# Graph network on one Trainium2 core: two edge stages regrouped into visits of 128-edge pairs, with unrolled gathers and an early fetch

## What is computed

```python
x = layernorm(x + L0(x))     # 4 rounds: segment_sum(x[src], dst), MLP with batch norms
x = layernorm(x + L1(x))     # edge MLP
x = layernorm(x + L2(x))     # 3 rounds of softmax aggregation (genconv)
x = layernorm(x + L3(x))     # continuous-filter interaction
# L1, per edge:  h = relu([x[src], x[dst], edge_attr_64] @ W1.T + b1)
#                agg = segment_sum(h @ W2.T + b2, dst);  then a two-layer node update
# L3, per edge:  Wij = (softplus(edge_attr_20 @ W_f.T + b_f) - log 2) * edge_weight
#                agg = segment_sum((x @ W_in.T + b_in)[dst] * Wij, src)
#                out = softplus(agg @ W_out.T + b_out) - log 2
```

## Time and profile before

| | |
|---|---|
| median of 3 runs | 3607.83 us (3603.68 to 3612.74) |
| profiled execution, its own time | 3592.89 us |
| its span, first to last instruction | 3591.2 us |
| prepare, adjacency and gin, up to the first layer norm | 0 to 741 us |
| edge_mlp: setup, loop, node update | 768 to 800, 800 to 1650, 1650 to 1702 us |
| genconv and its layer norm | 1725 to 2595 us |
| interaction: setup, loop | 2595 to 2661, 2661 to 3540 us |
| PE / DVE / ACT / POOL busy share of the span | 77% / 45% / 28% / 50% |

### The profile page before, as it was taken

The page is one execution under the profiler, slowest core; times in us unless marked ns, Lnnn a source line. Parts: engine busy times, 40 slices in busy tenths (PEclk is TensorE's granted clock), DMA queues, the critical chain, the costliest instruction groups (busy, mean ns, idle before and its releaser), DMA issues. The chain is left out here.

```text
span 3591.2 us, 51132 instructions
## 1 busy us (share of the span) xinstructions
PE 2767.2 (77%) x11270; PEld 1734.4 (48%) x11271; DVE 1627.7 (45%) x4686; ACT 999.8 (28%) x1815; POOL 1795.6 (50%) x1780
## 2 busy tenths in 40 slices
PE   3677788878999999998798899799636666666665
PEld 1233444457777777774444454354423333333333
DVE  7999222233333333332346436436524444444444
ACT  1333122221111111111110311211225454554543
POOL 2000000007777777772575475477037777777772
PEclk9999877765555555556899899899755555555556
DMA  0000000012222222221111011011021111111111
GB/s 7 3 0 0 20 0 0 0 49 55 53 53 54 55 53 53 54 54 38 31 17 12 11 17 13 10 17 17 28 87 35 35 35 35 35 35 35 35 35 32
DMA packets 181949, 108.52 MB, mean 30 GB/s; under 512 B 140291, under 2 KB 164066, under 8 KB 181148
## 3 DMA queue, kind: packets, MB, share of 16 engines
q0 software_dynamic: 88960, 66.98, 9.0%
q1 hardware_dynamic: 91662, 40.38, 4.4%
q10 hardware_dynamic: 1296, 0.79, 0.1%
HBM read 93.22 MB, written 13.33 MB: 30 GB/s over the span
## 5 line engine op out<-in xcount | busy, mean ns | idle before, releaser
L1720 POOL DMA_INDIRECT adj<-h_rows,adj x468 | 599.1, 1280 | 243.6 <-POOL adj L1716 124.9
L947 POOL DMA_INDIRECT work<-p_rows,work x468 | 569.4, 1217 | 242.8 <-POOL work L943 124.9
L1556 PE MATMUL ps<-adj,small 125*128 (+1 forms) x3150 | 631.5, 357 | 0.0
L1283 POOL DMA_INDIRECT edge_rows<-pay,small x425 | 513.6, 1208 | 129.2 <-issue 128.6
L1857 PE MATMUL ps<-adj 125*128 125x125 f32 x948 | 257.0, 442 | 313.1 <-DVE adj L1760 313.1
L1556 PEld LDWEIGHTS ps<-adj,small 125*128 125x128 bf16 x3150 | 311.5, 99 | 274.9 <-issue 12.6
L1857 PEld LDWEIGHTS ps<-adj 125*128 125x128 f32 x948 | 214.0, 326 | 399.2 <-DVE adj L1760 287.9
L1094 PE MATMUL ps<-small 64*125 64x128 f32 x936 | 337.2, 457 | 0.0
L928 POOL IOTA work<- 125x25 f32 x1 | 0.2, 154 | 656.7 <-POOLq L98 656.7
L986 DVE TENSOR_TENSOR work<-ps,work 125x384 f32<-125x384 f32 x156 | 87.1, 558 | 458.7 <-PE ps L1094 339.3
L1102 PE MATMUL ps<-work 125*128 125x125 f32 x936 | 249.3, 436 | 42.3 <-ACT work L1033 42.1
(11 more groups left out here) (318 smaller groups left out, 3727.4 us busy)
## 6 DMA issues: line engine op xcount, KB each, us to landing
small<-edge_attr SPq DMA_DIRECT2D x156, 93.8 KB
work<-p_rows,work POOLq DMA_INDIRECT x468
adj<-h_rows,adj POOLq DMA_INDIRECT x468, 3.4
edge_rows<-pay,small POOLq DMA_INDIRECT x425, 2.6
adj<-edge_rows SPq DMA_DIRECT2D x5, 996.1 KB
pay<-edge_pay SPq DMA_DIRECT2D x106, 46.9 KB
x_kept<-work SPq DMA_DIRECT2D x2, 1562.5 KB, 8.7
work<-x_kept SPq DMA_DIRECT2D x2, 1562.5 KB, 6.6
```

What stands on the lines that cost most here:

```text
L947: eng.indirect_dma_start(gathered[h][:, k * D:(k + 1) * D], None, p_rows[:, :], bass.IndirectOffsetOnAxis(ap=idx[h][:, k:k + 1], axis=0)). ...
L1283: eng.indirect_dma_start(edge_rows[:, :], bass.IndirectOffsetOnAxis(ap=place[:, k:k + 1], axis=0), pay[:, k * ROW:(k + 1) * ROW], None).th ...
L1556: ins = eng.matmul(ps[:, j, 0:cw], parts[k][:, i * D:(i + 1) * D], cols, start=first and i == 0, stop=last and i == 2, skip_group_check=True)
L1720: eng.indirect_dma_start(gathered[h][:, k * D:(k + 1) * D], None, h_rows[:, :], bass.IndirectOffsetOnAxis(ap=idx[h][:, k:k + 1], axis=0)). ...
```

## The change

- **Chunks, pairs, visits.** Edges are now in chunks of 128 (EW), two chunks make a pair (208 pairs, PAIRS). A *visit* is one pair with one node tile; a pair that touches two tiles is visited twice. Their number is fixed: 208 + 49 - 1 = 256 visits (VISITS) in edge_mlp with node tiles of 64 (MW, 49 of them), 208 + 25 - 1 = 232 (EDGE_VISITS) in interaction with tiles of 125. A word per visit (tile and pair) is computed at the start of each stage and read from SBUF by DVE, PE and SP with `value_load` at every visit. The tables of `prepare` (`ranges`) and its bin ends go.
- **One flat loop.** `quads_of` runs 4 visits (KB) per turn; the two-level loops `walk` and `units` go.
- **Gathers.** POOL's loop is written out, 208 pairs with 2 indirect DMAs each, the indices read straight from SBUF: no copy of indices, no wait for one. A ring of 4 pairs (edge_mlp) or 8 (interaction); POOL signals a pair's arrival two pairs later.
- **edge_mlp arithmetic.** The one-hot matrix by node and the edge features are stacked in one 128-row operand (`kmat`): SP fetches the targets of a pair broadcast over 64 partitions and the features under them, DVE turns the upper half into ones and zeros with one comparison, PE needs one matmul per chunk against the stacked weights (`qw`). The transposes, their copies, the bf16 splits and ACT's widening go. DVE adds each visit's sum into `R`.
- **interaction arithmetic.** Softplus as max(z, 0) + log(1 + exp(-|z|)), with exp and log from one ACT table; SP copies the edge rows of a visit; DVE adds each visit's sum into `S`.
- **Early fetch.** The layer norm ahead of interaction now fetches `edge_rows` (two transfers of 128 partitions, on SP and ACT) and the stage's weights. `h_rows` is written from two queues.

The core of the diff:

```diff
-            def body(w, c, q, opens):
-                for h in HALVES:
-                    if not first_of_all(q):
-                        eng.wait_ge(s_add[h], q)
-                        eng.nop(nofuse=True)
-                    eng.tensor_copy(idx[h], src_i[:, bass.ds(c + h * UH, UH)]).then_inc(s_idx[h], 1)
-                    eng.wait_ge(s_idx[h], q + 1)
-                    eng.nop(nofuse=True)
-                    for k in range(UH):
-                        eng.indirect_dma_start(gathered[h][:, k * D:(k + 1) * D], None, p_rows[:, :],
-                                               bass.IndirectOffsetOnAxis(ap=idx[h][:, k:k + 1], axis=0)
-                                               ).then_inc(s_g[h], 16)
+            for g in range(PAIRS + LAG):
+                if g < PAIRS:
+                    if g >= RING:
+                        n = eng.value_load(done[0:1, g - RING:g - RING + 1], min_val=1, max_val=VISITS)
+                        eng.wait_ge(s_add, nc.s_assert_within(n, 1, VISITS) + 2)
+                        eng.nop(nofuse=True)
+                    for k in range(PAIR):
+                        at = (g % RING * PAIR + k) * D
+                        c = g * PAIR + k
+                        eng.indirect_dma_start(gathered[:, at:at + D], None, p_rows[:, :],
+                                               bass.IndirectOffsetOnAxis(ap=src_i[:, c:c + 1], axis=0)
+                                               ).then_inc(s_g[g % RING], 16)
+                if g >= LAG:
+                    eng.wait_ge(s_g[(g - LAG) % RING], 16 * PAIR * ((g - LAG) // RING + 1))
+                    eng.nop(nofuse=True).then_inc(s_gd, 1)
...
+            def hots(v, b, word, i):
+                g, w = pair_of(word), tile_of(word)
+                eng.wait_ge(s_km[b], i)
+                eng.nop(nofuse=True)
+                eng.tensor_scalar(kmat[b][0:MW, :], kmat[b][0:MW, :].bitcast(I32), node_id[:, bass.ds(w, 1)], None,
+                                  ALU.is_equal).then_inc(s_ht, 1)
+                eng.wait_ge(s_tot, v + 1)
+                eng.nop(nofuse=True)
+                for k in range(PAIR):
+                    ins = eng.tensor_scalar(hot[b % 2][:, k * MW:(k + 1) * MW], iota, tile_lo[:, bass.ds(w, 1)],
+                                            dst_f[:, bass.ds(g * PAIR + k, 1)], ALU.add, ALU.is_equal)
+                ins.then_inc(s_hot, 1)
+            def add(v, b, word):
+                g = pair_of(word)
+                eng.wait_ge(s_gd, g + 1)
+                eng.wait_ge(s_prod, v + KB + 1)
+                eng.wait_ge(s_tot, v + 1)
+                eng.nop(nofuse=True)
+                eng.tensor_tensor(rows[b % 2], PROD[b % 2],
+                                  gathered[:, bass.ds((g & (RING - 1)) * (PAIR * D), PAIR * D)],
+                                  ALU.add).then_inc(s_add, 1)
+            def collect(v, b, word):
+                w = tile_of(word)
+                eng.wait_ge(s_tot, v + 3)
+                eng.wait_ge(s_r, v + 2)
+                eng.nop(nofuse=True)
+                r = R[:, bass.ds(w * MW, MW)]
+                eng.tensor_tensor(r, r, SUM[b % 2], ALU.add).then_inc(s_r, 1)
+            def body(v0, first, end):
+                words = {0: load_visit(eng, v0)}
+                if first:
+                    hots(0, 0, words[0], 32)
+                else:
+                    words[-1] = load_visit(eng, v0 - 1)
+                for b in range(KB):
+                    v = v0 + b
+                    if b < KB - 1 or not end:
+                        words[b + 1] = load_visit(eng, v + 1)
+                        n = (v0 // KB if isinstance(v0, int) else v0 >> 2) + (b + 1) // KB
+                        hots(v + 1, (b + 1) % KB, words[b + 1], n * 32 + 32)
+                    add(v, b, words[b])
+                    if b or not first:
+                        collect(v - 1, (b - 1) % KB, words[b - 1])
...
+            def hots(v, b, word):
+                g, w = pair_of(word), tile_of(word)
+                eng.wait_ge(s_tot, v + 1)
+                eng.nop(nofuse=True)
+                eng.tensor_scalar(rel[b], row3[:, bass.ds(g * PAIR, PAIR), SRC_C], tile_lo[:, bass.ds(w, 1)], None,
+                                  ALU.subtract).then_inc(s_rel, 1)
...
+            def message(v, b, word):
+                g = pair_of(word)
+                eng.wait_ge(s_ln, v + 1)
+                eng.nop(nofuse=True)
+                eng.scalar_tensor_tensor(soft[b], PROD[b], 0.0, soft[b], ALU.max, ALU.add).then_inc(s_sp, 1)
+                eng.wait_ge(s_sp, v + KB + 1)
+                eng.wait_ge(s_gd, g + 1)
+                eng.nop(nofuse=True)
+                eng.scalar_tensor_tensor(msg[b], soft[b], -LOG2,
+                                         gathered[:, bass.ds((g & (SLOTS - 1)) * (PAIR * D), PAIR * D)],
+                                         ALU.add, ALU.mult).then_inc(s_msg, 1)
...
+            if fetch:
+                fetch_rows(G, fetch, eng, 0, s_fetch)
+                eng.wait_ge(s_fetch, 16 * 8)
...
+            if fetch:
+                fetch_rows(G, fetch, eng, 1, s_fetch)
...
+            eng.wait_ge(s_spare, 2)
+            eng.dma_start(edge_rows.rearrange("(p c) f -> p c f", p=EW)[E % EW:EW, PAIR * PAIRS - 1, :],
+                          spare).then_inc(s_spared, 16)
+            eng.wait_ge(s_spared, 16)
```

More of the change, by code:

```diff
@@ L130, in build @@
         phase(genconv)
-        phase(layernorm)
-        phase(interaction)
+        rows = interaction_store(G)
+        phase(layernorm, fetch=rows)
+        phase(interaction, rows)
         phase(layernorm)
         phase(store)
-def load_range(nc, eng, ranges, row, w, steps, size):
-    word = eng.value_load(ranges[0:1, bass.ds(w + NT * row, 1)], min_val=0, max_val=(NC << 8) + steps)
-    return nc.s_assert_within(word >> 8, 0, NC), nc.s_assert_within(word & 255, 1, steps)
-class Passed:
-    def __init__(self, nc, eng, steps):
-        self.nc, self.eng, self.top = nc, eng, NT * steps
-        self.register = eng.alloc_register(f"steps_{nc.get_next_instruction_name()}")
-        eng.reg_mov(self.register, 0)
-    def now(self):
-        return self.nc.s_assert_within(self.eng.snap(self.register, min_val=1, max_val=self.top), 1, self.top)
-    def add(self, steps):
-        self.eng.reg_add(self.register, self.register, steps)
 def first_of_all(q):
@@ new lines, in total, with body @@
+            def total(v, b):
+                eng.wait_ge(s_hot, v + 1)
+                eng.wait_ge(s_relu, v + 1)
+                eng.wait_ge(s_r, v + 1)
+                eng.nop(nofuse=True)
+                for k in range(PAIR):
+                    ins = eng.matmul(SUM[b % 2], rows[b % 2][:, k * D:(k + 1) * D], hot[b % 2][:, k * MW:(k + 1) * MW],
+                                     start=k == 0, stop=k == PAIR - 1)
+                ins.then_inc(s_tot, 1)
+            def body(v0, first, end):
+                if first:
+                    products(0, 0)
+                for b in range(KB):
+                    if b < KB - 1 or not end:
+                        products(v0 + b + 1, (b + 1) % KB)
+                    total(v0 + b, b)
@@ L1591, in _, with interaction_store @@
                 eng.nop(nofuse=True).then_inc(s_fin, 1)
-def interaction(G):
-    nc, a, sem, work, small, ranges, ident, ps, T = (
-        G[k] for k in ("nc", "a", "sem", "work", "small", "ranges", "ident", "ps", "T"))
-    h_rows, edge_rows = G["h_rows"], G["edge_rows"]
+def interaction_store(G):
+    free = Words(G["adj_words"])
+    rows_t = free(EW, PAIR * PAIRS * ROW)
+    last, done = free(TP, 2, I32), free(1, PAIRS, I32)
+    w_in, b_in, w_out, b_out = free(D, D), free(EW, D), free(D, D), free(D, 1)
+    return dict(free=free, rows_t=rows_t, last=last, done=done, w_in=w_in, b_in=b_in, w_out=w_out, b_out=b_out)
@@ new lines, in collect, with body @@
+            def collect(v, b, word):
+                w = tile_of(word)
+                eng.wait_ge(s_tot, v + KB + 1)
+                eng.wait_ge(s_r, v + 2)
+                eng.nop(nofuse=True)
+                r = S[:, bass.ds(w * P, P)]
+                eng.tensor_tensor(r, r, SUM[b % 2], ALU.add).then_inc(s_r, 1)
+            def body(v0, first, end):
+                words = {}
+                if not first:
+                    words = {k: load_visit(eng, v0 + k) for k in (-2, -1)}
+                for b in range(KB):
+                    v = v0 + b
+                    words[b] = load_visit(eng, v)
+                    hots(v, b, words[b])
+                    message(v, b, words[b])
+                    if b >= 2 or not first:
+                        collect(v - 2, (b - 2) % KB, words[b - 2])
+                if end:
+                    for b in (2, 3):
+                        collect(v0 + b, b, words[b])
@@ L1817, in _, with body @@
+            def body(v0, first, end):
+                if first:
+                    attributes(0, 0)
+                    attributes(1, 1)
```

(9 more changed lines are left out.)

917 lines of the change are left out of this document (447 added, 470 removed).

## The result

The changed kernel takes 3739.1 us (median of 4 runs, 3737.17 to 3745.45) against 3607.8 before: ratio 1.0366, 95% interval 1.0348 to 1.0384. It is slower by 3.7%, and it lies above the range of the prediction. On a later occasion the ratio was 1.0381 (1.036 to 1.0402).

The account below looks back on a forecast made before the run. The prediction took POOL's stream to bound both loops before, PE also edge_mlp, and DVE's stream after. Its terms, +2 +15 -46 +3 +5 -6 = -27 us, gave 3580 us against 3607.8; range 3340 to 3700.

Parts of the forecast that it names:

- What bounds the kernel now: Before the change, POOL's instruction stream is full in both loops; in edge_mlp PE is full too, 805 of 850 us.
- POOL*'s term: Gather stream in both loops: 416 gathers in place of 468, 631 to 693 us, giving 219 and 222 us back.
- DVE becomes the long stream: edge_mlp's loop: DVE's reads and register work on every visit, 3.31 us x 256; 852 us against 850.
- Interaction: Interaction's loop: DVE's visit 3.45 us, 3.83 with the top of the turn, x 232; 894 us against 879.
- Setup of interaction and the layer norm: Ahead of interaction's loop: early fetch cuts the setup by 46 us; the layer norm that hides it grows by 3.
- Rest: Other stages: edge_mlp's setup +5 us for the table of visits, prepare -6 for about 30 small operations fewer.
- A: Both loops, slower: hand-overs cost more, 0.15 us per visit, 3653 us; up to 0.25, 3702; chance 0.30.
- B: Both loops, faster: DVE's register work runs beside the engine, 3130 us, or 3359 if only in edge_mlp; chance 0.15.
- C: Both loops: a contended load of a word takes 0.6 us, +0.45 per visit, 3800 us; chance 0.03.
- D: No difference: the early fetch only moves its cost into the third layer norm, 3596 to 3608 us; chance 0.05.

Follow-up runs that it names:

- before_128: Kernel before, its gathers fetching 128 rows in place of 125 (three unused rows) in edge_mlp and interaction: 3429.0 us, ratio 0.9525.
- fetch_alone: Changed kernel, with the early fetch moved into a stage of its own between the layer norm and interaction: 3720.0 us.
- half_gathers: Changed kernel without the second gather of each pair in edge_mlp, from the fifth pair on: the stretch with edge_mlp lasted 1025.4 us.
- lean: Changed kernel, DVE's words split once and kept, over the end of a turn too, without DVE's range checks on them: 3436.1 us, ratio 0.9572.
- more_reads: Changed kernel with one more, unused read of a word by DVE in every visit of both loops: 4039 us.
- carry: Changed kernel, DVE keeping the words of its last two visits in registers over the end of a turn, in both loops: 3641.8 us, ratio 1.0102.
- gather_sizes: Changed kernel, edge_mlp's gathers fetching eleven numbers of rows in turn, from 128 to 32: 3773 us.
- gather125: Changed kernel, edge_mlp's gathers fetching 125 rows in place of 128: 3814 us.

## Why the prediction was wrong

**What bounds the kernel now** was right, and before_128 shows it: cheaper gathers alone took 175 us off, interaction by 137, and edge_mlp came to rest on PE.

***POOL*'s term** was wrong in size, without effect on the time. I carried 1.217 and 1.280 us over to gathers of 128 rows, "may cost 2% more", and bounded the stream by 631 to 693 us. A gather of 128 rows took 0.946: 416 x (0.946 + 0.30) = 518 us. The rule on divisors stood further down in my own text, applied to the fetch alone. Since DVE bounds both loops, the 113 us too much in edge_mlp and 139 in interaction stayed hidden; in a kernel bound by gathers this would have been the largest term, as before_128 shows.

***DVE becomes the long stream*:** the mechanism was right, the size off at one place, the register work at the top of a turn. The visit was put at 3.05 us and took 3.09. The top of the turn was put at 1.5, of which a slack of 0.45 would cover a part, +1.05; it took 1.79. The timeline shows how: from L1009 to L984 there are 3.28 us over the top and 1.40 elsewhere, so the two reads and the branch cost 1.9. Of the slack only 0.2 to 0.3 us are there (the wait ahead of L989), and most of that is lost again to register work ahead of the add, 0.33 at the top. 63 x (1.79 - 1.05) = 47 us; 256 x 0.04 = 10; the first add comes 11.9 us after the first gather where I gave 5, 7 us (in fetch_alone and half_gathers it comes after 7.5, so 4 of these aren't the change's). Together 64, of the 65 by which that stretch missed.

***Interaction*:** the same at the top, 1.71 in place of 1.5, which is 12 us. More came from the visit, 3.75 in place of 3.45 (232 x 0.30 = 70 us). Read off the visit shown above, its parts are: relation and its wait 0.44 (put at 0.36), comparisons 0.52 (0.54), the combination with the hand-over 0.79 (0.77), dispatch of the second product and of the add into S 0.53 (0.30), read and register work 1.48 (1.43 and 0.05). The last two together are 1.92 to 2.08 at the three places inside a turn, where I had 1.78. The failed step is the dispatch: ahead of each engine instruction stand a wait, its address and mostly a range check, and I counted about half of these. The third term is the start of the loop:

```profile
2708.46 0.43 DVE L1787 SCALAR_TENSOR_TENSOR adj<-adj 128x256 f32<-128x256 f32 x1 [0.38 <-DVE adj L1783]
...
2717.23 0.43 DVE L1787 SCALAR_TENSOR_TENSOR adj<-adj 128x256 f32<-128x256 f32 x1 [4.49 <-issue]
...
2730.51 0.42 DVE L1787 SCALAR_TENSOR_TENSOR adj<-adj 128x256 f32<-128x256 f32 x1 [0.38 <-DVE adj L1783]
```

Two visits took 22.0 us where two later ones take 7.6, 14 us more. 12 + 70 + 14 = 96, where the stretch missed by 93. This term isn't DVE's register work: in fetch_alone and half_gathers, with the same loop, the same two distances are 3.14 and 3.12 us, and the loop's stretch is 15 to 16 us shorter. What holds the engines up there in the other profiles stays open.

**Setup of interaction and the layer norm** together: -45 against -43. The fetch lasts 18 us and is hidden whole; I had left 3 us for it.

**Rest:** prepare -4 against -6, edge_mlp's setup +8 against +5.

**The rivals.** *A* had the right sign and a price that was too low: 0.15 us per visit, at most 0.25, where the sum fell short by 0.22 in edge_mlp (0.04 + 0.74/4) and 0.35 in interaction (0.30 + 0.21/4). Its mechanism, instructions between the engine's own that I hadn't counted, is the dispatch of interaction; the reads at the top are the other part. The visits came to 3.54 and 4.18 us on average, over the 3.4 and 3.95 that I had named as its sign. *B* fell: a little register work does run beside the engine, but the reads do so only while the add of 0.2 to 0.3 us lasts, and one more read cost 0.58 to 0.63 of its 0.72 us. (Its 3130 takes 37 us for the parts outside the loops, where the sum has 44: 3123.) Even with most of that work gone (lean) the loops came to 813 and 806 us, not to POOL's 631 and 657. *C* fell: a read took 306 ns in the median with four engines reading. The Trainium skill ("DMA: Bandwidth & Descriptors", "Latency and other measured facts") gives a floor of about 600 ns; for a read from SBUF the trace differs, and the measurement decides. What a read costs here is 0.72 us all the same, with the register instructions behind it. *D* fell: the setup gave 45 us.

The step that failed in both loops is thus the same, the count of DVE's register instructions: 1.79 us net at edge_mlp's top where it had 1.05, and 0.30 us more per visit of interaction. lean, which takes nothing but such instructions away, is the run that shows it. The range ended at 3700 since its upper end was A's at the same estimates per instruction. Both loops missed the same way, so the two errors added.

## What to carry to other kernels

In a loop whose engine instructions last 0.2 to 0.5 us, count the sequencer's instructions of the engine with the longest stream, at their pitch (0.06 to 0.1 us each, 0.7 for a read with its checks), as closely as the engine's own; a flat loop with one word per visit pays this on every visit, and cutting it (keep words in registers, split them once, leave the range checks out) gave 7 to 8% with no change to the arithmetic. And look at the partition count of every gather and transfer before restructuring anything: three more rows per gather, which nothing reads, brought the kernel before to 0.9525 of its time, as far as the whole rewrite came with its register work cut (0.9572).

## What the runs showed that I had not expected

A gather's time on POOL follows the largest divisor up to 16 of its rows far more than its size: 952 ns for 128, 865 for 32, 1195 for 125, 2551 for 127.

On some occasions single register instructions take 0.55 to 0.8 us. In edge_mlp's loop SP's stream had 191 and 202 of them in the two profiles of the changed kernel, and 118 to 197 in the other changed kernels of the first and third group. The profiles of the second group (lean, half_gathers, fetch_alone) had none. The third group has them on the same chip number, 13. The long genconv and the slow start of interaction's loop come and go with them.

On SP, which has time, they cost little: from the first add of edge_mlp's loop to its last 901 us passed in the changed kernel and 898 in fetch_alone. On DVE they cost their length. Its stream in edge_mlp's loop had 6 and 5 in the changed kernel, 20 in more_reads and 26 in carry, 39 in gather_sizes and 88 in gather125. The two with gathers of other than 128 rows have the most, but one profile of each doesn't show that the gathers bring them; the cause stays open.
